# A fused attention and mixture-of-experts kernel: the front's transfers, a burst of products of constants, and the turning of maxima two exponentials later

## The reference

```
scores = einsum('bsqhd,bthd->bqhst', qh, kh) * scale
probs  = softmax(scores, axis=-1)
a_dot  = einsum('bqhst,bthd->bsqhd', probs, vh)
a_mem  = (elu(q) @ memory) / (elu(q) @ memory_norm)
out    = a_dot * (1 - w) + a_mem * w
```

## Time and profile before

| | us |
|---|---|
| runs | 755.53, 756.81, 758.07 (median 756.81) |
| the profiled execution | 757.83 |
| its span, from the first instruction to the last | 755.7 |
| PE busy | 714.2 (95%) |
| DVE busy | 596.4 (79%) |
| ACT busy | 492.1 (65%) |
| POOL busy | 133.2 (18%) |

### The profile page before, as it was taken

The page is one execution under the profiler, slowest core; times in us unless marked ns, Lnnn a source line. Parts: engine busy times, 40 slices in busy tenths (PEclk is TensorE's granted clock), DMA queues, the critical chain, the costliest instruction groups (busy, mean ns, idle before and its releaser), DMA issues.

```text
span 755.7 us, 16796 instructions
## 1 busy us (share of the span) xinstructions
PE 714.2 (95%) x5000; PEld 394.1 (52%) x5001; DVE 596.4 (79%) x1056; ACT 492.1 (65%) x886; POOL 133.2 (18%) x282
## 2 busy tenths in 40 slices
PE   5999999899999999999999989899999999999998
PEld 2455544622222222222222222488888888888887
DVE  5366489899999999999999984377777877767764
ACT  1473600298888889888898888656566566556332
POOL 1000000666531111111111111000000000004750
PEclk9999999999999999999999999989999999999999
DMA  9728200177411110011111182041111111132431
GB/s 315 259 69 301 79 0 1 33 233 230 154 61 33 32 33 25 25 33 33 33 32 26 37 268 92 15 147 49 55 42 55 56 48 49 56 98 71 126 110 51
DMA packets 49955, 65.42 MB, mean 87 GB/s; under 512 B 8168, under 2 KB 42880, under 8 KB 49920
## 3 DMA queue, kind: packets, MB, share of 16 engines
q1 hardware_dynamic: 38560, 40.58, 17.0%
q10 hardware_dynamic: 8288, 15.99, 6.6%
q0 software_dynamic: 3072, 8.39, 3.5%
HBM read 40.15 MB, written 24.38 MB: 85 GB/s over the span
## 4 chain that ended last, share of the span: by engine, by line
PE 78%; DVE 7%; issue 6%; POOL 4%; ACT 3%; DMA 1%; SPq 0%; ACTq 0%; POOLq 0%; DVEq 0%
PE ps L1409 14%; PE ps L1378 12%; PE ps L1477 9%; PE ps L1433 8%; PE ps L1258 8%; PE ps L1511 6%; DVE smax L1008 5%; PE ps L1282 5%; PE ps L1250 3%; PE ps L1526 3%; PE ps L1468 2%; PE ps L1218 2%; ACT o_sb L696 1%; PE ps L1215 1%; PE ps L1363 1%
## 5 line engine op out<-in xcount | busy, mean ns | idle before, releaser
L1008 DVE TENSOR_REDUCE smax<-ps 128x1 f32<-128x512 f32 x512 | 311.6, 679 | 17.1 <-PE ps L1282 17.1
L737 ACT ACTIVATE att<-ps 128x512 f32<-128x512 f32 x512 | 275.2, 595 | 40.8 <-PE ps L1433 32.3
L1378 PE MATMUL ps<-att,v_head 128*32 128x256 f32 x2048 | 164.4, 393 | 13.0 <-ACT o_sb L696 12.7
L1433 PE MATMUL ps<-att 51*128 51x512 bf16 x512 | 159.4, 384 | 3.4 <-ACT att L737 1.3
L1282 PE MATMUL ps<-att 48*128 48x512 bf16 x512 | 158.2, 383 | 0.0
L1409 PE MATMUL ps<-att_r 128*128 128x512 f32 x456 | 120.0, 413 | 2.8 <-DVE att_r L1069 2.8
L1065 DVE TENSOR_TENSOR att_r<-big,att_r 128x1024 fp32r<-128x1024 f32 x76 | 90.4, 1229 | 24.4 <-ACT att_r L717 23.8
L1409 PEld LDWEIGHTS ps<-att_r 128*128 128x128 f32 x456 | 87.1, 192 | 21.8 <-DVE att_r L1069 3.3
L1433 PEld LDWEIGHTS ps<-att 51*128 51x128 bf16 x512 | 37.8, 93 | 114.3 <-DVE smax L1008 64.5
L1378 PEld LDWEIGHTS ps<-att,v_head 128*32 128x32 f32 x2048 | 40.6, 108 | 100.2 <-issue 57.7
L717 ACT ACTIVATE att_r<-big 128x1024 fp32r x74 | 74.3, 1052 | 18.7 <-issue 18.7
(11 more groups left out here) (165 smaller groups left out, 698.4 us busy)
## 6 DMA issues: line engine op xcount, KB each, us to landing
big<-w ACTq DMA_DIRECT2D x8, 1024.0 KB
q_stacks<-big SPq DMA_DIRECT2D x12, 512.0 KB
att<-q_stacks SPq DMA_DIRECT2D x64, 96.0 KB
slot_x<-zeros SPq DMA_DIRECT2D x1, 4992.0 KB, 17.5
e_x<-slot_x SPq DMA_DIRECT2D x39, 128.0 KB, 2.0
slot_y<-xn SPq DMA_DIRECT2D x39, 128.0 KB, 1.7
big<-w ACTq DMA_DIRECT2D x8, 512.0 KB
att<-k_stacks SPq DMA_DIRECT2D x64, 48.0 KB
```

The lines of the kernel that those rows point to most:

```text
L737: act.activation(probs[:, t % 2, g, :], ps[:, RING[turn_of(u) % 3], :], ACT.Exp, scale=SCALE)\
L1008: dve.reduce_max(smax[:, s % 2, 8 * half + v:8 * half + v + 1], ps[:, bank + half, :], X_AXIS)\
L1378: last = pe.matmul(ps[32 * g:32 * (g + 1), 6, queries], v_head[:, s % 2, t, :], probs[:, t % 2, g, queries], start=s % 2 == 0 and t == 0 a ...
L1433: pe.matmul(ps[:, RING[turn % 3], :], k_st[s][rows, P * t:P * (t + 1)], q_st[s][rows, g, :], start=True, stop=True).then_inc(scores_ready, 1)
```

## The change

Five things are edited.

1. The transfers at the start. The first group of x comes as four transfers of 128 rows, two issued by SP and two by ACT, each with a semaphore of its own, and DVE waits for them tile by tile. ACT issues the projection weights and the router's too. The first projection no longer waits for the router's transfer.
2. Products of constants. Before anything else PE runs 18 products of the 128x128 bf16 identity with a 128x512 tile of ones into bank 7, whose content is overwritten later. POOL fills the tile of ones earlier for that.
3. ACT's square root for group n + 1 stands directly behind the two copies of group n. The logits and turned values use other PSUM banks, and three waits in front of `shared_group(0)` move behind its first pair of products.
4. `MAX_AT` is 6 and not 4: PE turns the maxima at the end of round 2 and no longer of round 1; ACT copies the pair's outputs in front of exponential 4 (was 5) and the turned maxima in front of exponential 6 (was 4).
5. The multiplication of the reciprocals by 1 - w goes from DVE (without the wait in front of it) to POOL, at the head of `add_o`.

The core of the diff:

```diff
-        TURNS, MAX_AT, OUT_AT = 18, 4, 13
+        TURNS, MAX_AT, OUT_AT = 18, 6, 13
...
+        WARM = 18
...
-            for n in range(4):
+            for c in (0, 2):
+                sp.dma_start(acc[:, c, :], x_rows[P * c:P * (c + 1), :]).then_inc(x_first[c], 16)
+            for n in range(1, 4):
                 sp.dma_start(acc[:, 4 * n:4 * n + 4, :],
                              x_rows[512 * n:512 * (n + 1), :].rearrange("(c p) d -> p c d", p=P))\
-                  .then_inc(x_loaded[n], 16)
...
+            pool.memset(ones[:, :], 1.0).then_inc(ones_ready, 1)
             pool.memset(router[:, :, :], 0.0).then_inc(router_zero, 1)
...
             def add_o(pair, a, b, h):
 
+                pool.wait_ge(rden_ready, pair + 1)
+                pool.tensor_tensor(rden[:, a, :], rden[:, a, :], mixw[:, 3:4].to_broadcast([P, 32]), ALU.mult)\
+                    .then_inc(rden_scaled, 1)
                 pool.wait_ge(rden_scaled, pair + 1)
...
+            for c in (1, 3):
+                act.dma_start(acc[:, c, :], x_rows[P * c:P * (c + 1), :]).then_inc(x_first[c], 16)
+            act.dma_start(wkv_sb[:, :, 0:DKV], wkT.rearrange("(k p) n -> p k n", p=P)).then_inc(proj_loaded, 16)
+            act.dma_start(wkv_sb[:, :, DKV:2 * DKV], wvT.rearrange("(k p) n -> p k n", p=P)).then_inc(proj_loaded, 16)
+            act.dma_start(wq_sb, wqT.rearrange("(k p) n -> p k n", p=P)).then_inc(proj_loaded, 16)
+            act.wait_ge(router_zero, 1)
+            act.dma_start(router[:, :, 0:E], router_w.rearrange("(k p) n -> p k n", p=P)).then_inc(router_loaded, 16)
...
+            sqrt_var(0)
             for n in range(4):
-                sqrt_var(n)
                 copy_xT(2 * n)
                 copy_xT(2 * n + 1)
+                if n < 3:
+                    sqrt_var(n + 1)
...
-                    if u == 4 and not last:
+                    if u == MAX_AT and not last:
                         negate_max(i + 1, s + 1, blk * 2 + (s + 1) // 2)
...
-                        if u == 5:
+                        if u == 4:
                             evacuate_o(blk * 2 + (s // 2 - 1), (s // 2 + 1) % 2)
...
                 dve.reciprocal(rden[:, a, :], o[:, :, DH]).then_inc(rden_ready, 1)
-                dve.wait_ge(rden_ready, pair + 1)
-                dve.tensor_scalar_mul(rden[:, a, :], rden[:, a, :], mixw[:, 3:4]).then_inc(rden_scaled, 1)
...
+            pe.wait_ge(eye_ready, 1)
+            pe.wait_ge(ones_ready, 1)
+            for _ in range(WARM):
+                pe.matmul(ps[:, 7, :], eye[:, :], ones[:, :], start=True, stop=True)
...
-                    pe.wait_ge(proj_loaded, 64)
+                    pe.wait_ge(proj_loaded, 48)
...
+                        if f == 1:
+                            pe.wait_ge(v_copied, 2)
+                            pe.wait_ge(logits_copied, 1)
+                            pe.wait_ge(qk_copied, 12)
...
-                    if t == MAX_AT // G - 1 and not last:
-                        transpose_max(i + 1, s + 1)
+                        if v == MAX_AT // 2 - 1 and not last:
+                            transpose_max(i + 1, s + 1)
```

More of the change, by code:

```diff
@@ L202, in build @@
         gath = xnf.rearrange("p (a w n) -> p a w n", a=2, w=8)
-        x_loaded = [sem(f"x_loaded{n}") for n in range(4)]
+        x_first = [sem(f"x_first{c}") for c in range(4)]
+        x_loaded = [sem(f"x_loaded{n}") for n in range(1, 4)]
         proj_loaded = sem("proj_loaded")
+        router_loaded = sem("router_loaded")
         small_loaded = sem("small_loaded")
@@ L496, in _ @@
             pool.memset(zeros[:, :], 0.0)
-            pool.memset(v_head[:, :, :, :], 0.0)
-            link(pool.memset(ones[:, :], 1.0))
+            link(pool.memset(v_head[:, :, :, :], 0.0))
             for a in range(2):
@@ L638, in _ @@
             act.wait_ge(lT_in_psum, 1)
-            act.activation(o_sb[:, 0, :], ps[:, 1, :], ACT.Copy).then_inc(lT_copied, 1)
-            for half, bank in enumerate((0, 3)):
+            act.activation(o_sb[:, 0, :], ps[:, 4, :], ACT.Copy).then_inc(lT_copied, 1)
+            for half, bank in enumerate((5, 1)):
                 act.wait_ge(v_in_psum, half + 1)
@@ L858, in _ @@
                 part = slice(4 * n, 4 * n + 4)
-                dve.wait_ge(x_loaded[n], 16)
+                if n > 0:
+                    dve.wait_ge(x_loaded[n - 1], 16)
                 for c in tiles:
+                    if n == 0:
+                        dve.wait_ge(x_first[c], 16)
                     last = dve.bn_stats(stats[:, c, :], acc[:, c, :])
@@ L1224, in _ @@
                 if n == 0:
-                    pe.wait_ge(proj_loaded, 64)
+                    pe.wait_ge(proj_loaded, 48)
                 for u in range(*UNITS[n]):
                     project_qk(u)
+            pe.wait_ge(router_loaded, 16)
+            pe.wait_ge(qk_copied, 9)
             for k in range(KD):
                 for g in range(4):
-                    last = pe.matmul(ps[32 * g:32 * (g + 1), 1, :], router[:, k, :], xnT[:, k, 512 * g:512 * (g + 1)],
+                    last = pe.matmul(ps[32 * g:32 * (g + 1), 4, :], router[:, k, :], xnT[:, k, 512 * g:512 * (g + 1)],
                                      start=k == 0, stop=k == KD - 1)
@@ L1235, in _ @@
             for c in range(NT):
-                last = pe.transpose(ps[:, 3 * (c // 8), DKV * (c % 8):DKV * (c % 8 + 1)],
+                last = pe.transpose(ps[:, 5 - 4 * (c // 8), DKV * (c % 8):DKV * (c % 8 + 1)],
                                     kv[DKV:2 * DKV, P * c:P * (c + 1)], ident[DKV:2 * DKV, DKV:2 * DKV])
@@ L1241, in _ @@
             for t in range(4):
-                last = pe.transpose(ps[:, 2, P * t:P * (t + 1)], o_sb[:, 0, P * t:P * (t + 1)], ident[:, :])
+                last = pe.transpose(ps[:, 3, P * t:P * (t + 1)], o_sb[:, 0, P * t:P * (t + 1)], ident[:, :])
             last.then_inc(logits_in_psum, 1)
```

14 lines of the change are left out of this document (4 added, 10 removed).

## The result

The changed kernel takes 736.95 us (median of 6 runs, 736.45 to 737.31), the one before 756.62 (6 runs, 755.53 to 758.07): a ratio of 0.974, 95% interval 0.9727 to 0.9752. I had said 742.2 with a range from 737.0 to 750.5, so the time lies 5.2 us under the forecast and just outside the range. The profiled execution took 736.45 us against 757.83.

| us | before | after | less | forecast |
|---|---|---|---|---|
| to the first maximum of attention | 147.59 | 144.65 | 2.94 | 2.9 |
| to the first reciprocal | 28.43 | 27.50 | 0.93 | |
| 12 pairs, reciprocal to reciprocal | 248.06 | 235.83 | 12.23 | |
| the 13th pair | 21.93 | 20.90 | 1.03 | 11.1 for these three |
| to the first of the experts' products | 36.04 | 34.04 | 2.00 | 0.6 |

A forecast was written before the change was run, and what follows sets the result against it. DVE was taken to bound attention, stalled by ACT's order through PE, and PE the front, at its lower clock. Terms 2.9 + 3.8 + 6.8 + 1.1 = 14.6 us, off 756.81, gave 742.2 us, range 737 to 750.5.

The forecast's parts named there:

- PE's wait for the copy: Sign in attention: PE's wait for ACT's copy of a pair's outputs at about 0.35 us instead of 0.81.
- the short stall: DVE's idle time of 0.24 us in each pair, while PE turns the outputs; forecast to stay.
- the burst's end: Sign at the start: PE's 18 products of constants end at about 9.0 us, between 6.2 and 10.1.
- The front: Term before attention: faster turning and first projection units after the products of constants, 2.9 us less.
- The reciprocal: Term in attention: DVE without the multiplication and its wait saves 0.27 us in each of 14 pairs, 3.8 us.
- Copy and turn: Term in attention: earlier copy of outputs, later turning of maxima; 0.52 us in each of 13 pairs, 6.8 us.
- DVE's long stall: DVE's idle time in round 3 of an even step, 0.57 us in the mean, of which 0.52 goes.
- The end: Step 30, where DVE has no maxima and PE's waiting of 0.97 us is the path: 0.6 us less.
- Both stalls go: Rival in attention: PE also covers the turning of the outputs, 3.1 us more gained, 739.1 us; 15%.
- No new wait of PE: Rival in attention: PE waits for exponential 5 or negated maxima instead of the copy, 750.1 us; 15%.
- the rows of maxima: Rival at each step's first score: these rows arrive too late and PE waits, 25 us slower, 767 us; 4%.
- The front gives nothing: Rival at the start: burst runs too long or the lower clock returns after the pause, 745.6 us; 15%.

The follow-up runs named there:

- the second six runs: The changed kernel run again unaltered, beside three edits of it: median 738.6 us, ratio 0.9736 to the kernel before.
- the profile without the burst: The changed kernel without PE's 18 products of constants, the other edits of the front kept: median 739.69 us.
- copy and turn: The kernel before with only ACT's copy of the outputs moved ahead and the maxima turned a round later: 742.89 us, ratio 0.9814.
- the copy alone: The kernel before with only ACT's copy of the outputs put ahead of the negated maxima, both at exponential 4: 744.28 us, ratio 0.9828.
- the reciprocals alone: The kernel before with only the reciprocals' multiplication moved from DVE to POOL: 756.11 us, ratio 0.9978.
- the front alone: The kernel before with only the new front, the other edits undone: 755.97 us, ratio 0.9975.

## Why the prediction was wrong

The direction was right, and so were most of the signs that I had named: PE's wait for the copy at 0.34, the reciprocal followed by a maximum after 0.26, the short stall still there, the burst's end at 9.15, the logits at 35.00. But the pairs became 19.63 and not 19.9, and the gain is 19.7 us, in the second six runs 19.1 (738.6 beside 757.7), where I had 14.6.

**The front** came out as forecast: 2.94 for 2.9, first unit at 11.19 for 11.0, logits at 35.00. That is in part luck. I gave all of it to the burst and nothing to the other edits, and by the profile without the burst they brought 0.34 by an earlier start and up to 0.9 more that may be scatter. My sum had a slip as well: from 17.7 to 14.4 are 3.3 us and not 3.1. The moved waits gave nothing, as said: the first maximum comes exactly as much sooner as the logits.

**The reciprocal** was right in its place and wrong in its worth. It is followed by a maximum after 0.26, as forecast. The Trainium skill (VectorE: DVE Perf Modes, section "The DRAIN you can't avoid") says that the pipeline empties behind each operation, except that a next operation that is not held starts earlier, and that a semaphore between two costs nothing more, which it measured on copies. The 0.26, which is less than the reciprocal's own record of 0.34, agrees with the earlier start; that the semaphore costs nothing does not fit here, since with the wait the next maximum starts 0.46 after the reciprocal. But the 3.8 us were DVE's time, not the kernel's. Alone they gave nothing in 12 pairs (248.06, 248.19), with at most 1.5 lost to POOL's parts; behind copy and turn 1.4 (237.27, 235.83).

**Copy and turn** were worth almost twice their term: 10.8 us in 12 pairs, where I had 6.2. This is the step that failed. I wrote "ACT's order ends the wait, and DVE pays for it", and then priced the copy's move by DVE's long stall alone (0.52 of 0.57 in a pair) and held the short one fixed ("nothing there changes, so it stays"), as if DVE's work and its stalls could each be taken away by itself. PE's wait for the copy was behind both: with the copy alone moved, PE's 9.8 us of waiting for it are gone, DVE's stalls go from 9.8 to 0.8, the short one with the long one, and 12 pairs are 9.7 us shorter, 0.81 each, which is that wait in full. PE's other wait, for POOL's parts in the odd step, I had read the earlier trace rows and used only to cover POOL's product; it was worth little, for the copy alone left its 5.5 us in place, and taking them away by the later turning brought 1.1 more. A second, smaller slip: an idle time is listed from the end of a record, and maxima overlap by 0.08, so a stall of 0.57 costs 0.65. I had hidden that in 0.604 us for each maximum, where the rows give 0.598.

**The two errors** had opposite signs, if copy and turn are taken first: reciprocals 3.8 forecast, about 1.4 found; copy, turn and first pair 7.3 forecast for the stretch, about 12.8 found (14.2 less 1.4). With the reciprocals first they gave nothing and the rest all of it, so the split depends on the order. The sum missed by 3.1 us there. Read on DVE's rows of before and after, the changed pair looks as I had added it up, reciprocal and long stall gone and the short stall left, at 0.27 and 0.65 (I had 0.52): 11.0 of the 12.23 us; the rest is in no listed stall.

**The end.** The stretch from the 13th reciprocal to the experts gave 2.0 and not 0.6. In the kernels with the reciprocals alone and with the front alone, which kept the order of copy and turn, it takes 35.03 and 35.11 against 36.04 before, at a clock of 1.0 where before had 0.69 (459 to 464 us, behind the wait of the earlier trace rows); so about 1.0 is the clock. The other 1.0 is as much as PE's listed waits fell there: from 1.9 with the reciprocals alone (0.8 for the copy, 0.6 for POOL's parts, 0.5 for xn) to 0.9 (0.7 for the copy, 0.2 for an exponential). The 2.17 us in the experts are no gain of the change: in the second profile of the same kernel this stretch takes 274.75, more than before, 2.47 of it in the row shown above. The range left no room for that, though the runs of before spread over 2.5 us.

**The rivals.** "Both stalls go" is what copy and turn do by themselves; the shorter reciprocal brings the short stall back. No new wait of PE for exponential 5 or the negated maxima is listed in the 12 pairs, and no score waits for the rows of maxima beyond one step, as in the earlier trace rows. "The front gives nothing" by the clock falling in the pause happened in part, in one profile of nine: with the copy one exponential sooner the turning behind the burst took 1.04 us and the first unit, after the 2.03 us of waiting, 2.58, at a granted clock of 0.75 from 10.8 to 13.3 us. Two figures of mine were off without bearing on the sum: 13 x 0.57 is 7.4 and not 7.5, and a pair that is 0.8 shorter makes a step 0.4 shorter and not 0.7, so 5.9 us and not 5.6 were left for the rows of maxima.

**What stays open:** why what PE gains in round 2 doesn't reach the outputs' turning, why the shorter reciprocal brings the short stall back, and how much of the 1.2 us beside the burst is the edits' and how much scatter.

## What to carry to other kernels

When two engines feed each other through a few buffers and both are busy for over 90%, don't add up one engine's work and stalls: list the waits of both over the same stretch, and price an edit by the waits that it takes from the engine whose waits are named (here 15.4 us on PE), since time taken from the other turns into stalls. That price holds only down to the other engine's own work: with the copy moved, a pair was 19.87 against DVE's 19.71, PE's remaining 5.5 us for POOL's parts were worth 1.1, and in the changed kernel 2.0 us less of PE's waits gave nothing. Where runs of one kernel spread by more than their pairs or stages differ, look for a wait behind which a product takes twice its time, and leave room for it in the range.

## What the runs showed of the hardware

- A wait of DVE for its own last instruction costs 0.20 us here (0.46 against 0.26 between the starts of a reciprocal and a maximum).
- After the same wait of 2.78 us the same twelve products took 3.02 us in some profiles and 5.49 in others (granted clock 1.00 and 0.77 over 15 us), and 4.34 to 4.58 in three. With 12 products of constants in the wait they took 3.02 and 3.04 in the two profiles, and the runs spread over 1.3 and 1.5 us; those of the changed kernel itself, over 0.9 and 4.3.
- The burst's products follow one another every 0.43 us at first and every 0.22 later; 18 of them took 5.36 to 6.94 us in different profiles, so where the clock rises isn't the same in each execution.
